# Next image's projection three steps later in a state-space loop, and attention's row-of-maxima matmuls issued pair by pair

## The chip, the cores and the metric

The kernel runs on one core of a Trainium2 chip. The metric is the device time of one execution in microseconds (us). The engines are TensorE (PE in the profile, its weight loads PEld), VectorE (DVE), ScalarE (ACT), GpSimd (POOL) and SyncE (SP), which here only issues DMAs. Each engine works through its own instruction stream and waits on counting semaphores.

## The reference

A tensor x of 16 images, 64 channels, 32x32 pixels passes four blocks. The change touches the first and the last.

```python
# block 0: transformer, 8 heads of 32, 1024 tokens per image
qkv = layer_norm(x_flat, g1, beta1) @ w_qkv.T
scores = jnp.einsum('bhqd,bhkd->bhqk', q, k) * HEAD_DIM ** (-0.5)
attn = jax.nn.softmax(scores, axis=-1)
out = jnp.einsum('bhqk,bhkd->bhqd', attn, v)
...
# blocks 1 and 2: two 3x3 convolutions with batch norm, then iterative whitening
...
# block 3: state space model, 128 channels, 16 states, L = 1024
xz = jnp.einsum('blc,ec->ble', xn, W_in); xi, z = jnp.split(xz, 2, axis=-1)
xc = jax.nn.silu(causal depthwise conv of xi, 4 taps)
dt, Bm, Cm = jnp.split(jnp.einsum('bld,ed->ble', xc, W_x), ...)
delta = jax.nn.softplus(dt @ W_dt.T + b_dt)
hst = hst * exp(d_t A) + (d_t * u_t) B_t;  y_t = sum over n of hst C_t
out = ((ys + xc * Dp) * silu(z)) @ W_out.T + x
```

## The kernel before

The program is a chain of phases, each a block with one hand-written stream for each engine. Two phases matter here: attention and state space.

**Attention.** The work is cut into 32 periods (16 images, two groups of four heads), each of 16 steps: two halves of 512 queries by eight blocks of 128 keys. A step works on a 128-key block and 512 queries for the four heads of a group. The heads lie on partitions 0-31, 32-63, 64-95 and 96-127, so a matmul of head h uses rows 32h to 32h+31 of TensorE's array. In step s TensorE issues:

- `scores` (lines 391 to 403): for each head the float32 product K·Q into PSUM tile `at_sc` (line 398; the profile records each such matmul as two passes), and then for each head a one-row bf16 matmul of ones by `at_nrow` (line 401), which adds the negated row maximum to all scores. Before head 0 it waits until the exponential of heads 0 and 1 of the step before is done (`exp_done`), and before head 2 for that of heads 2 and 3, since `at_sc` is not doubled. `sc_ready` is raised after the ones matmul of head 1 and again after that of head 3.
- `maxima`, heads 0 and 1 (line 334), which make bf16 scores for the maxima of a later group, in a ring of three PSUM banks that VectorE reduces (line 526);
- in some steps, other units in the same ring: projections of q and k (steps 0 and 1), the turning of maxima into rows (4 and 12), projections of v (6), softmax denominators (1 and 9);
- `values`, the product of the probabilities of step s-1 with V (line 410), and `maxima` of heads 2 and 3.

ScalarE takes the exponential of two heads at a time (line 479, `at_sc` to `at_probs`), first heads 0 and 1, then heads 2 and 3.

**State space.** Per image there are 16 steps n, one for each state. VectorE scans in two halves (lines 1587, 1591) and multiplies by the spread row of C (`see`, line 1599). TensorE spreads row n of C over 128 partitions (line 1411, PSUM tile `ss_C`, one buffer, so it waits for `see` of n-1) and adds the seen state of n-1 into `ss_Y` (line 1423). ScalarE makes the decay (line 1534), GpSimd the drive (line 1634).

The next image's inputs are made within the same 16 steps by four units of TensorE in `unit(b + 1, ...)`, each issued between the C row of step n and the `ss_Y` matmuls behind it. A table of step numbers (line 1278) sets where: `AT_X` for unit 0, the projection and convolution of the next image (line 1388, from `ss_xn` and `ss_w_taps` into PSUM tile `ss_aux`), and for ScalarE's `take_x` (line 1463), which copies it out; `AT_Z` (8) for unit 1, the gate (line 1393), `AT_BC` (9), `AT_DT` (12) and so on. `AT_CONV` is in the table but is read nowhere. Unit 0 waits for `xn_in`, the two DMAs of `ss_xn`. SyncE issues these in step `TURN` (3), behind the store of the image before, which waits for `res_done` of ScalarE in step 2:

```python
                if n == TURN:
                    sp.wait_ge(gate_done, b + 1)
                    load_x(b + 1)
```

Of the kernel before, what the change touches and what calls it, by code (L numbers as in the profile page):

```python
# [19 lines left out]
HEADS, DH = 8, 32  # L20
INNER = HEADS * DH
GH = P // DH
# [125 lines left out]
def attention_phase(nc, sem, xn_d, wqkvT, ident_bf, attn_d):  # L148
# [39 lines left out]
    def stage_before(stage, grp):  # L188
        if stage == "first":
            return "lead"  # L190
        return "first" if isinstance(grp, int) and grp == 1 else "mid"
# [7 lines left out]
    def unit_count(stage, grp, unit):  # L199
        is_max = unit[1] == "max"  # L200
        same = [u for u in UNITS[stage] if (u[1] == "max") == is_max]
        return counted_before(N_MAX if is_max else N_EXTRA, grp) + same.index(unit) + 1

    def unit_of(stage, kind, which, s=None):
        return next(u for u in UNITS[stage] if u[1:3] == (kind, which) and s in (None, u[0]))
# [12 lines left out]
    with ExitStack() as ctx:  # L218
# [6 lines left out]
        ones_bf = sb("at_ones_bf", [P, P], BF16)  # L225
# [9 lines left out]
        nrow = sb("at_nrow", [P, 2, HALF], BF16)  # L235
# [3 lines left out]
        sc = ps("at_sc", [P, GH, HALF])  # L239
# [10 lines left out]
        def hs(h):  # L250
            return slice(h * HALF, (h + 1) * HALF)

        def blk(k):
            return slice(k * P, (k + 1) * P)

        def head(h):
            return slice(h * DH, (h + 1) * DH)
# [54 lines left out]
        def _(pe):  # L312
# [76 lines left out]
            def scores(stage, grp, par, s):  # L389
                half, kb = divmod(s, KB)  # L390
                if kb == 0:

                    at = stage if half else stage_before(stage, grp)
                    pe.wait_ge(extra_done, unit_count(at, grp if half else grp - 1, unit_of(at, "turn", half)))
                for h in range(GH):
                    if h % 2 == 0 and not (stage == "first" and s == 0):
                        pe.wait_ge(exp_done, 2 * (STEPS * grp + s - 1) + h // 2 + 1)
                    nc.tensor.matmul(sc[:, h, :], KT[head(h), par, blk(kb)], QT[head(h), par, hs(half)], start=True, stop=False)  # L398
                for h in range(GH):
                    row = slice(h * DH, h * DH + 1)  # L400
                    m = nc.tensor.matmul(sc[:, h, :], ones_bf[row, :], nrow[row, half, :], start=False, stop=True)  # L401
                    if h % 2:
                        m.then_inc(sc_ready, 1)

            def values(grp, par, s):
# [8 lines left out]
            def period(grp, par, stage):  # L414
                for s in range(STEPS):
                    if stage != "lead":
                        scores(stage, grp, par, s)
                    maxima(stage, grp, par, s, (0, 1))
                    if s < 2:
                        project(stage, grp, par, s)  # L420
                    if s % KB == 1 and stage != "lead":
                        denominators(stage, grp, 1 - s // KB)
                    if s == 4 or s == 12:
                        turn(stage, grp, 1 if s == 4 else 0)
                    if s == 6:
                        values_projected(stage, grp, par)
                    if stage != "lead":
                        if s == 0:
                            if stage != "first":
                                values(grp - 1, 1 - par, STEPS - 1)  # L430
                        elif s % KB == 2:
                            values(grp, par, s - 2)
                            values(grp, par, s - 1)
                        elif s % KB != 1:
                            values(grp, par, s - 1)
                    maxima(stage, grp, par, s, (2, 3))
# [769 lines left out]
def state_space_phase(nc, sem, xn_d, xw_d, w_inT, conv_w, conv_b, w_xT, w_dtT, b_dt, a_log, d_p, w_outT,  # L1206
# [15 lines left out]
    with ExitStack() as ctx:  # L1222
# [52 lines left out]

        LEAD = DEPTH - 2

        AT_X, AT_CONV, AT_Z, AT_BC, AT_REST, AT_MID, AT_DT, AT_LOW, AT_DELTA = 3, 4, 8, 9, 10, 11, 12, 12, 13

        def loop_steps(b, par):  # L1280

# [389 lines left out]
def conv_transformer_ssm(nc, a, out):  # L1671

    with ExitStack() as ctx:
# [23 lines left out]
        with nc.sbuf_tensor("x_centred", [P, PAIRS, S], F32) as centred:  # L1697
            whitening_phase(nc, sem, x2_d, total, a["pair_m"], a["mask_m"], a["ident"], centred, wm)
            whiten_norm_phase(nc, sem, centred, wm, a["L2_conv_weight"], a["L2_conv_bias"], a["L3_conv_ln_w"],
                              a["L3_conv_ln_b"], a["mean_m"], xw_d, xm_d)  # L1700
        state_space_phase(nc, sem, xm_d, xw_d, a["L3_conv_W_in"], a["L3_conv_conv_w"], a["L3_conv_conv_b"],
                          a["L3_conv_W_x"], a["L3_conv_W_dt"], a["L3_conv_b_dt"], a["L3_conv_A_log"], a["L3_conv_Dp"],
                          a["L3_conv_W_out"], a["select_m"], a["ident"], rows_d, out.rearrange("n c h w -> n c (h w)"))
# [37 lines left out]
```

## Time and profile before

| | us |
|---|---|
| median of 3 runs | 3976.04 |
| lowest and highest | 3971.3 and 3979.86 |
| the profiled execution, own time | 3973.87 |
| its span (first to last instruction) | 3972.2 |
| TensorE busy | 3373.5 (85%) |
| VectorE busy | 2573.4 (65%) |
| ScalarE busy | 2001.1 (50%) |
| GpSimd busy | 1924.1 (48%) |

The busy time of TensorE counts overlapping matmuls once and stretches with a lower clock, so it does not say that the array is full. The mean granted clock of TensorE was 0.917 of the full 2.4 GHz.

### The profile page before, as it was taken

How to read it: one execution, taken by the hardware profiler on the slowest of the kernel's cores; microseconds unless marked ns; L12 is line 12 of the kernel's file. 1: busy time of each engine (PE TensorE's matmuls, PEld its weight loads, DVE VectorE, ACT ScalarE, POOL GpSimd, SP SyncE). 2: the span in 40 equal slices, each digit the busy share in tenths (PEclk: the TensorE clock that was granted, in tenths of full speed). 3: DMA queues.
4: the chain of work that ended last, by engine and by line, in shares of the span. 5: the costliest groups of instructions: out<-in, count | busy, mean ns of one | idle time of the engine just before them, and what ended most of it. 6: DMA issues, size and time to landing. Idle time of an engine off the chain costs nothing. (4 is left out here: it accounts for less than half of the span.)

```text
span 3972.2 us, 56517 instructions
## 1 busy us (share of the span) xinstructions
PE 3373.5 (85%) x19062; PEld 1207.9 (30%) x19062; DVE 2573.4 (65%) x3346; ACT 2001.1 (50%) x2381; POOL 1924.1 (48%) x620
## 2 busy tenths in 40 slices
PE   6999999999999999999995999657777777777777
PEld 2333333333333333333331333422222222222222
DVE  5677677676676776767750222237777777777777
ACT  3566566565565665656652333234454445444554
POOL 0555566555565655556653000016555655555555
PEclk7899999999999999999997999778888888888888
DMA  2000000000000000000003210134323332333242
GB/s 95 12 14 15 10 17 15 15 15 10 15 17 15 9 15 15 15 15 12 15 9 92 90 63 16 56 103 146 136 96 139 115 130 96 139 115 128 96 143 102
DMA packets 74768, 235.22 MB, mean 59 GB/s; under 512 B 13089, under 2 KB 14181, under 8 KB 74421
## 3 DMA queue, kind: packets, MB, share of 16 engines
q1 hardware_dynamic: 69460, 215.06, 16.0%
q0 software_dynamic: 5056, 16.83, 1.2%
q8 instruction: 155, 2.54, 0.3%
q14 instruction: 97, 0.79, 0.1%
HBM read 192.42 MB, written 39.39 MB: 58 GB/s over the span
## 5 line engine op out<-in xcount | busy, mean ns | idle before, releaser
L526 DVE TENSOR_REDUCE at_pmax<-at_ring 128x1 f32<-128x512 f32 x2048 | 1305.1, 685 | 512.5 <-PE at_ring L334 511.6
L479 ACT ACTIVATE at_probs<-at_sc 128x1024 f32<-128x1024 f32 x1024 | 992.5, 1021 | 660.4 <-PE at_sc L401 660.3
L580 POOL TENSOR_TENSOR at_prob_sums<-at_prob_sums,at_probs 128x2048 f32<-128x2048 f32 x192 | 869.3, 4527 | 109.7 <-ACT at_probs L479 98.7
L398 PE MATMUL at_sc<-at_QT,at_KT 32*128 32x512 f32 x4096 | 847.8, 642 | 21.9 <-issue 21.6
L1634 POOL TENSOR_TENSOR ss_drive<-ss_du,ss_bsb 128x1024 f32<-128x1024 f32 x261 | 610.0, 2350 | 424.9 <-DVE ss_state L1591 417.8
L580 POOL TENSOR_TENSOR at_prob_sums<-at_probs 128x2048 f32<-128x2048 f32 x64 | 291.0, 4547 | 791.2 <-ACT at_probs L479 791.2
L410 PE MATMUL at_O<-at_probs,at_V 128*32 128x512 f32 x4096 | 539.2, 610 | 53.0 <-DVE at_att L549 51.8
L1534 ACT ACTIVATE ss_decay<-ss_delta,ss_a 128x512 f32<-128x512 f32 x520 | 353.2, 687 | 441.8 <-DVE ss_state L1587 304.0
L1423 PE MATMUL ss_Y<-ss_seen,ss_ident 128*128 128x512 f32 x1032 | 540.1, 649 | 0.0
L1599 DVE TENSOR_TENSOR ss_seen<-ss_state,ss_C 128x1024 f32<-128x1024 f32 x259 | 316.3, 1221 | 256.4 <-PE ss_C L1411 249.8
L334 PE MATMUL at_ring<-at_KH,at_QH 32*128 32x512 bf16 x2048 | 447.4, 389 | 5.7 <-DVE at_pmax L526 2.9
L1591 DVE TENSOR_TENSOR_SCAN ss_state<-ss_decay,ss_state,ss_drive 128x512 f32<-128x512 f32 x259 | 332.2, 1283 | 31.5
L401 PE MATMUL at_sc<-at_nrow,at_ones_bf 1*128 1x512 bf16 x2048 | 339.5, 381 | 0.0
L1587 DVE TENSOR_TENSOR_SCAN ss_state<-ss_decay,ss_drive 128x512 f32<-128x512 f32 x259 | 314.8, 1215 | 22.3 <-POOL ss_drive L1634 15.8
L398 PEld LDWEIGHTS at_sc<-at_QT,at_KT 32*128 32x128 f32 x4096 | 274.9, 186 | 176.2 <-ACT at_probs L479 149.2
L1411 PE MATMUL ss_C<-ss_bc,ss_select 96*128 96x512 bf16 x518 | 167.0, 406 | 188.6 <-DVE ss_seen L1599 187.5
L334 PEld LDWEIGHTS at_ring<-at_KH,at_QH 32*128 32x128 bf16 x2048 | 150.9, 92 | 534.1 <-DVE at_pmax L526 342.9
L1423 PEld LDWEIGHTS ss_Y<-ss_seen,ss_ident 128*128 128x128 f32 x1032 | 208.4, 206 | 241.2 <-issue 192.0
L1388 PE MATMUL ss_aux<-ss_xn,ss_w_taps 128*128 128x512 f32 x136 | 104.7, 941 | 109.6 <-DMA ss_xn<-scratch_xm 108.6
L385 PE MATMUL at_ring<-at_probs,at_ones 128*32 128x512 f32 x1512 | 175.3, 596 | 1.4 <-DVE at_pmax L526 1.4
L938 POOL DMA_DIRECT2D scratch_x<-fc_out x8 | 4.3, 534 | 351.6 <-ACT fc_out L839 351.6
L410 PEld LDWEIGHTS at_O<-at_probs,at_V 128*32 128x32 f32 x4096 | 87.6, 108 | 273.2 <-issue 189.3
(199 smaller groups left out, 2728.2 us busy)
## 6 DMA issues: line engine op xcount, KB each, us to landing
ss_bsb<-scratch_rows SPq DMA_DIRECT2D x265, 512.0 KB, 6.8
scratch_attn<-at_att SPq DMA_DIRECT2D x64, 256.0 KB, 2.0
fc_att<-scratch_attn SPq DMA_DIRECT2D x32, 512.0 KB, 5.8
ss_xn<-scratch_xm SPq DMA_DIRECT2D x34, 256.0 KB, 5.5
at_xn<-scratch_xn SPq DMA_DIRECT2D x32, 256.0 KB, 3.8
ss_xw<-scratch_xw SPq DMA_DIRECT2D x17, 256.0 KB, 3.7
ln_x<-in_x SPq DMA_DIRECT2D x8, 512.0 KB, 4.4
scratch_xn<-ln_xn POOLq DMA_DIRECT2D x8, 512.0 KB, 3.0
```

The lines of the kernel that those rows point to most:

```text
L334: nc.tensor.matmul(ring[:, unit[3], :], QH[head(h), p, blk(quad // 2)], KH[head(h), p, hs(quad % 2)], start=True, stop=True).then_inc(max_ ...
L398: nc.tensor.matmul(sc[:, h, :], KT[head(h), par, blk(kb)], QT[head(h), par, hs(half)], start=True, stop=False)
L401: m = nc.tensor.matmul(sc[:, h, :], ones_bf[row, :], nrow[row, half, :], start=False, stop=True)
L410: m = nc.tensor.matmul(O[head(h), :], V[:, par, kb, head(h)], probs[:, kb, h, :], start=(kb == 0), stop=(kb == KB - 1))
L479: nc.scalar.activation(probs[:, kb, two, :].rearrange("p h q -> p (h q)"), sc[:, two, :].rearrange("p h q -> p (h q)"), ACT.Exp, scale=SCA ...
L526: nc.vector.tensor_reduce(pmax[:, quad // 2, h, quad % 2:quad % 2 + 1], ring[:, unit[3], :], AX_X, ALU.max, negate=True).then_inc(max_done, 1)
L580: nc.gpsimd.tensor_tensor(prob_sums[:, half, :, :], before, probs[:, k, :, :], ALU.add).then_inc(pool_sums, 1)
L1423: m = nc.tensor.matmul(Y[:, hs(h)], ident[:], seen[:, n % DEPTH, hs(h)], start=False, stop=(n == N - 1))
L1534: nc.scalar.activation(decay[:, hs(h)], delta[:, par, hs(h)], ACT.Exp, scale=a_neg[:, n:n + 1])\
L1591: nc.vector.tensor_tensor_scan(now[:, hs(1)], decay[:, hs(1)], drive[:, n % DEPTH, hs(1)], now[:, HALF - 1:HALF], ALU.mult, ALU.add).then_ ...
L1599: nc.vector.tensor_tensor(seen[:, n % DEPTH, :], state[:, n % 2, :], Cp[:], ALU.mult).then_inc(seen_done, 1)
L1634: nc.gpsimd.tensor_tensor(drive[:, n % DEPTH, :], du[:, par, :], bsb[:, n % SLOTS, :], ALU.mult).then_inc(drive_done, 1)
```

## The change

In attention, the ones matmuls of heads 0 and 1 are issued right behind the scores of heads 0 and 1, ahead of the wait for heads 2 and 3 and of their scores; before, all four came behind all four scores. In the state space phase, `AT_X` goes from 3 to 6: unit 0 of TensorE and `take_x` of ScalarE for the next image move three steps later. `AT_CONV` changes too, without effect. SyncE's stream is the same.

```diff
                     if h % 2 == 0 and not (stage == "first" and s == 0):
                         pe.wait_ge(exp_done, 2 * (STEPS * grp + s - 1) + h // 2 + 1)
                     nc.tensor.matmul(sc[:, h, :], KT[head(h), par, blk(kb)], QT[head(h), par, hs(half)], start=True, stop=False)
-                for h in range(GH):
-                    row = slice(h * DH, h * DH + 1)
-                    m = nc.tensor.matmul(sc[:, h, :], ones_bf[row, :], nrow[row, half, :], start=False, stop=True)
                     if h % 2:
+                        for of in (h - 1, h):
+                            row = slice(of * DH, of * DH + 1)
+                            m = nc.tensor.matmul(sc[:, of, :], ones_bf[row, :], nrow[row, half, :], start=False, stop=True)
                         m.then_inc(sc_ready, 1)
...
-        AT_X, AT_CONV, AT_Z, AT_BC, AT_REST, AT_MID, AT_DT, AT_LOW, AT_DELTA = 3, 4, 8, 9, 10, 11, 12, 12, 13
+        AT_X, AT_CONV, AT_Z, AT_BC, AT_REST, AT_MID, AT_DT, AT_LOW, AT_DELTA = 6, 6, 8, 9, 10, 11, 12, 12, 13
```

TensorE's stream in attention, the steps around an early period's turning unit, as it was (`at_sc` is scores, `at_ring` the ring, `at_O` the output):

```order
38 L401 MATMUL at_sc<-at_nrow,at_ones_bf 128x512 x4
39 L334 MATMUL at_ring<-at_KH,at_QH 128x512 x2
40 L410 MATMUL at_O<-at_probs,at_V 32x512 x4
41 L334 MATMUL at_ring<-at_KH,at_QH 128x512 x2
42 L398 MATMUL at_sc<-at_QT,at_KT 128x512 x4
43 L401 MATMUL at_sc<-at_nrow,at_ones_bf 128x512 x4
44 L334 MATMUL at_ring<-at_KH,at_QH 128x512 x2
45 L372 MATMUL at_ring<-at_ident,at_negm 128x128 x4
```

The same place of TensorE's stream with the change:

```order
46 L402 MATMUL at_sc<-at_nrow,at_ones_bf 128x512 x2
47 L334 MATMUL at_ring<-at_KH,at_QH 128x512 x2
48 L410 MATMUL at_O<-at_probs,at_V 32x512 x4
49 L334 MATMUL at_ring<-at_KH,at_QH 128x512 x2
50 L398 MATMUL at_sc<-at_QT,at_KT 128x512 x2
51 L402 MATMUL at_sc<-at_nrow,at_ones_bf 128x512 x2
52 L398 MATMUL at_sc<-at_QT,at_KT 128x512 x2
53 L402 MATMUL at_sc<-at_nrow,at_ones_bf 128x512 x2
54 L334 MATMUL at_ring<-at_KH,at_QH 128x512 x2
55 L372 MATMUL at_ring<-at_ident,at_negm 128x128 x4
```

The number of matmuls is the same; two ones matmuls moved ahead of two scores.

TensorE's stream in the state space loop, from step 2 of an image to step 5, as it was (`ss_aux<-ss_xn,ss_w_taps` is unit 0):

```order
1539 L1423 MATMUL ss_Y<-ss_seen,ss_ident 128x512 x2
1540 L1429 REGISTER_ALU
1541 L1411 MATMUL ss_C<-ss_bc,ss_select 128x512 x2
1542 L1381 ISA
1543 L1388 MATMUL ss_aux<-ss_xn,ss_w_taps 128x512 x4
1544 L1423 MATMUL ss_Y<-ss_seen,ss_ident 128x512 x2
1545 L1429 REGISTER_ALU
1546 L1411 MATMUL ss_C<-ss_bc,ss_select 128x512 x2
1547 L1423 MATMUL ss_Y<-ss_seen,ss_ident 128x512 x2
```

The place where unit 0 now stands in TensorE's stream, steps 6 to 8 of the same image, with unit 1 (`ss_aux<-ss_xn,ss_w_in`) behind it:

```order
1742 L1411 MATMUL ss_C<-ss_bc,ss_select 128x512 x2
1743 L1381 ISA
1744 L1388 MATMUL ss_aux<-ss_xn,ss_w_taps 128x512 x4
1745 L1423 MATMUL ss_Y<-ss_seen,ss_ident 128x512 x2
1746 L1429 REGISTER_ALU
1747 L1411 MATMUL ss_C<-ss_bc,ss_select 128x512 x2
1748 L1423 MATMUL ss_Y<-ss_seen,ss_ident 128x512 x2
1749 L1429 REGISTER_ALU
1750 L1411 MATMUL ss_C<-ss_bc,ss_select 128x512 x2
1751 L1393 MATMUL ss_aux<-ss_xn,ss_w_in 128x512 x2
```

Unit 0 has moved behind three more pairs of C row and `ss_Y`; ScalarE's `take_x` moves past three steps of decays in the same way.

## Rows read from the trace of the kernel before

**Rows 1.** Busy time by window: attention, then state space; clock and DMA last.

```profile
core 0: us, PE busy (x) PEld busy (x) DVE busy (x) ACT busy (x) POOL busy (x), PEclk, DMA share, GB/s
95.00:2120.00 2025.00, 1917.06 (x15294) 672.51 (x15293) 1401.30 (x2261) 1194.00 (x1402) 1160.28 (x256) 0.98 0.04 14
2640.00:3972.00 1332.00, 986.57 (x2096) 353.94 (x2096) 982.51 (x817) 616.42 (x778) 725.97 (x312) 0.85 0.35 120
```

**Rows 2.** Waits in state space: total us, times, longest.

```profile
DVE ss_seen L1599 <- PE ss_C L1411: 244.4, 67, 10.6
PE ss_aux L1388 <- DMA ss_xn<-scratch_xm: 108.6, 15, 7.7
```

**Rows 3.** Timeline of one image around step 3: start, us, engine, instruction, idle before.

```profile
3251.15 0.60 PE L1411 MATMUL ss_C<-ss_bc,ss_select 96*128 96x512 bf16 x2
3252.30 1.12 SPq L1291 DMA_DIRECT2D ss_xn<-scratch_xm  x2
...
3259.13 6.34 PE L1388 MATMUL ss_aux<-ss_xn,ss_w_taps 128*128 128x512 f32 x8 [7.38 <-DMA ss_xn<-scratch_xm]
...
3267.02 0.60 PE L1411 MATMUL ss_C<-ss_bc,ss_select 96*128 96x512 bf16 x2
...
3267.72 1.22 DVE L1599 TENSOR_TENSOR ss_seen<-ss_state,ss_C 128x1024 f32<-128x1024 f32 x1 [10.47 <-PE ss_C L1411]
```

**Rows 4.** The first and the last such stall of VectorE, of 15.

```profile
2793.42 1.22 DVE L1599 TENSOR_TENSOR ss_seen<-ss_state,ss_C 128x1024 f32<-128x1024 f32 x1 [10.16 <-PE ss_C L1411]
...
3902.36 1.22 DVE L1599 TENSOR_TENSOR ss_seen<-ss_state,ss_C 128x1024 f32<-128x1024 f32 x1 [10.36 <-PE ss_C L1411]
```

**Rows 5.** Timeline of undisturbed steps, and unit 1 in step 8.

```profile
3275.30 1.22 DVE L1599 TENSOR_TENSOR ss_seen<-ss_state,ss_C 128x1024 f32<-128x1024 f32 x1
...
3279.10 1.22 DVE L1599 TENSOR_TENSOR ss_seen<-ss_state,ss_C 128x1024 f32<-128x1024 f32 x1
...
3280.91 3.20 PE L1393 MATMUL ss_aux<-ss_xn,ss_w_in 64*128 64x512 f32 x4
```

**Rows 6.** Timeline of the first image, whose `ss_xn` had landed before step 3.

```profile
2708.07 3.60 PE L1388 MATMUL ss_aux<-ss_xn,ss_w_taps 128*128 128x512 f32 x8
...
2711.51 1.88 PE L1423 MATMUL ss_Y<-ss_seen,ss_ident 128*128 128x512 f32 x4
...
2713.92 1.22 DVE L1599 TENSOR_TENSOR ss_seen<-ss_state,ss_C 128x1024 f32<-128x1024 f32 x1 [0.19 <-PE ss_C L1411]
```

**Rows 7.** Busy time by window after the stall; the granted clock is the number behind POOL.

```profile
3264.50:3281.50 17.00, 12.77 (x35) 5.01 (x34) 13.27 (x11) 6.47 (x10) 7.05 (x3) 1.00 0.06 22
3281.60:3288.30 6.70, 6.70 (x10) 1.89 (x8) 4.89 (x4) 5.93 (x7) 3.91 (x2) 0.50 0.00 0
```

**Rows 8.** Waits in attention: total us, times, longest.

```profile
ACT at_probs L479 <- PE at_sc L401: 623.6, 423, 9.3
```

**Rows 9.** Timeline of step 15 of an attention period.

```profile
1045.75 1.94 ACT L479 ACTIVATE at_probs<-at_sc 128x1024 f32<-128x1024 f32 x2 [1.24 <-PE at_sc L401]
...
1046.83 1.60 PE L398 MATMUL at_sc<-at_QT,at_KT 32*128 32x512 f32 x6
1047.73 0.19 PEld L398 LDWEIGHTS at_sc<-at_QT,at_KT 32*128 32x128 f32 x2 [0.60 <-ACT at_probs L479]
...
1047.80 0.38 PE L401 MATMUL at_sc<-at_nrow,at_ones_bf 1*128 1x512 bf16 x2
...
1048.27 0.59 PE L398 MATMUL at_sc<-at_QT,at_KT 32*128 32x512 f32 x2
...
1048.93 1.94 ACT L479 ACTIVATE at_probs<-at_sc 128x1024 f32<-128x1024 f32 x2 [1.24 <-PE at_sc L401]
```

**Rows 10.** Timeline of step 3, in which nothing makes TensorE wait.

```profile
1034.82 1.24 PE L398 MATMUL at_sc<-at_QT,at_KT 32*128 32x512 f32 x8
...
1036.20 1.94 ACT L479 ACTIVATE at_probs<-at_sc 128x1024 f32<-128x1024 f32 x2 [2.31 <-PE at_sc L401]
```

**Rows 11.** First scores of one period and of the next: the first and last of 17 starts.

```profile
1050.01 0.70 PE L398 MATMUL at_sc<-at_QT,at_KT 32*128 32x512 f32 x2
...
1111.47 0.70 PE L398 MATMUL at_sc<-at_QT,at_KT 32*128 32x512 f32 x2
```

## The prediction

> **What bounds the kernel now.** I first cut the span into stages [rows 1]: attention takes 2025 us, state space 1332 us, and each is half of the change. Then I read in each the list of waits and one timeline.
>
> State space. The list of waits shows VectorE waiting 244.4 us for the C row of TensorE, longest 10.6, and TensorE waiting 108.6 us in 15 waits for the DMA of `ss_xn` [rows 2]. The timeline joins the two [rows 3]. In step 3 the C row is out at 3251.15; next in the stream stands unit 0, and its data are asked for only at 3252.30. They land at 3259.13, after 7.38 us of an idle TensorE. The unit then takes 6.34 us. Only behind it and the `ss_Y` matmuls comes the next C row (3267.02), for which VectorE has sat 10.47 us. Undisturbed steps are 3.80 us apart (3275.30 to 3279.10) [rows 5], and there VectorE is the bound, with next to no gap. So a step of VectorE is the unit of time of this stage, and once an image 10.2 to 10.5 us are added. The first and the last stall show 10.16 and 10.36 [rows 4]; there are 15 of them, one for each image but the first. The sum of the 15 excesses over 3.80, from one first-half scan to the next, is 154 us (15 x 10.27).
>
> Attention. ScalarE waits 623.6 us for the ones matmuls, 423 times [rows 8]. A step is a closed loop [rows 9]. Let t be the start of the scores of head 0, u the start of those of head 2, e the start of the first exponential. The exponential of the step before starts at 1045.75, and u comes 1.98 later (1047.73), when its second half has freed the banks. The scores of heads 2 and 3 end at 1048.27 + 0.59 = 1048.86, and e is 1048.93, u + 1.20. But the ones matmuls of heads 0 and 1, all that the first exponential needs, had started at 1047.80 and ended at 1048.18. It is released 0.75 us later, right behind the last score, which stands ahead of them in program order: I read that ends are reported in program order. The loop is u to e 1.20, e to u 1.98: 3.18 us, the distance of the two ACT rows, with ScalarE idle for 1.24. Where TensorE never waits, e is 1.38 behind t (1034.82 to 1036.20) [rows 10].
>
> **Part 1, state space.** Nothing is added; unit 0 moves. At 3.80 us a step, see 3 starting at 3253.5 puts the C row of step 6 at about 3262.3 and the unit at 3262.8, against data landed at 3259.13: 3.7 us to spare, and the longest wait (7.7) [rows 2] is only 0.3 above the one shown. The DMA wait goes. SyncE's queue is unchanged, and so are the stores and row spreads behind the load.
>
> What is left is the unit's own work in a step whose bound is VectorE. The trace has this case: in the first image `ss_xn` had landed before step 3 [rows 6]. There the unit took 3.60 us, the `ss_Y` matmuls 1.88, and VectorE's next but one `see` waited 0.19 us. The step was 0.14 longer. So at full clock the stall costs 0.14 instead of 10.27.
>
> The clock is the unknown. Behind the stall the clock was 0.50 and the unit took 6.34 instead of 3.60; then 1.00 for 17 us of undisturbed steps, and 0.50 again for 6.7 us from 3281.6, over unit 1 (3.20 us) [rows 5, 7]. TensorE had then been through a few undisturbed steps, in which it pauses for VectorE (12.77 us busy of 17), since its last dense stretch; a unit in step 6 stands behind three such steps too. So I take one chance in two that a 6.8 us dip falls on it. Such a dip takes away half of its length in streaming, 3.4 us, of which 0.1 is slack: 3.3. Some of that returns, as the same dip no longer falls on units 1 and 2. I take 1.1 us net per image. Bounds: 0 (all at full clock) and 6.34 - 3.60 + 1.9 for `ss_Y` at half clock + 0.3 = 4.9 (none). Saved: 15 x (10.27 - 0.14 - 1.1) = 135 us; bounds 152 and 78.
>
> ScalarE's `take_x` moves too; ScalarE is busy for 6.47 of those 17 us [rows 7], and in the first image the same copy beside the same decays is inside the 0.14.
>
> **Part 2, attention.** No instruction is added. With the ones matmuls of heads 0 and 1 ahead of the scores of heads 2 and 3, the first exponential starts at t + 1.39 whatever u is, if ends are reported in order; and u of the next step becomes t + 1.39 + 1.98 = t + 3.37 to 3.39, where it was u + 3.18. What TensorE needs from u to the next t stays: 2.28 us in a plain step (1047.73 to 1050.01) [rows 9, 11], more where other units stand. Write d = u - t (0.90 now in plain steps; at least 0.22, since head 2 runs behind the maxima of heads 2 and 3) and w for the stretch from u to the next t. Then the step is d + w, and the next d is the larger of 0.22 and 3.39 - (d + w). Over the period shown, 1050.01 to 1111.47 = 61.46 us, the sixteen w, from the seventeen starts of which these are the first and last, are 4.48, 6.75, 4.02, 2.46, 2.85, 2.28, 4.26, 2.28, 2.28, 4.86, 4.03, 2.46, 2.85, 2.28, 2.28, 2.28: together 52.7. The d are 0.90, 0.22 three times, 0.70, 0.33, 0.90, 0.22, 0.88, 0.90, 0.22, 0.22, 0.70, 0.33, 0.90, 0.90: 8.76. By the rule the d become 0.89, 0.22 three times, 0.71, 0.22, 0.89, 0.22, 0.89, 0.22 three times, 0.71, 0.22, 0.89, 0.22: 7.18. A run of plain steps alternates 2.50 and 3.17, mean 2.83 instead of 3.18, but most of the period lies in steps that TensorE's other units set, where nothing is won. Saved: 1.58 us a period, 32 periods: 51 us. Next in line is TensorE itself, busy with w. Bounds: 0, with the loss as a rival below, and 64: w may shrink where it holds waits on the ring that ScalarE's earlier finish shortens; I allow 0.4 a period, 32 x 1.98.
>
> **Sum.** 135 + 51 = 186 off the profiled execution's own time, 3973.9 (2.2 below the median): 3788; with the 2 us of the median, 3790.
>
> **Rivals.**
>
> - *Attention slower than before.* Program order could hold starts as well as ends: the scores of head 2 would then start only behind the ones matmul of head 1, 0.97 behind t. With d never under 0.97 the period is 52.7 + 15.5 = 68.2, +6.8 x 32 = +216, less 135: 4055. It decides from d of about 0.8 in every step (+134). Against it: the ones matmuls that started at 1047.80 stand in program order behind the second passes of heads 2 and 3, which started at 1048.27 [rows 9]; different row groups overtake each other. Chance 0.04.
> The Trainium skill, page "TensorE: Matmul & The Clock Gate", section "The mechanism", has matmuls strictly first in, first out in start and end. By its rule for starts this rival would happen, and the time would be the one given above. The trace agrees with the rule for ends (released at 1048.93, not 1048.18) and contradicts that for starts (1047.80 before 1048.27), so the rows decide.
> - *Attention gains nothing.* A milder form: the weight load of the scores of head 2 queues behind that of the ones matmul, which waits for the second pass of head 0, about 0.54 behind t (as 1048.27 is behind 1047.73 for head 2). With d at least 0.55 the period is 61.5: no gain. For it: no row shows a ones load pending ahead of an unstarted score. Against it: loads of later rows in other row groups did go ahead. Total 3841. Chance 0.13.
> - *Half clock in most units 0*, or DMA lands late in some images: state space saves 78 to 100; total 3825 to 3850. Chance 0.10.
> - *The stall only moves.* If the loads were pushed back with the step, unit 0 would stall as before. The loads are issued in step 3 as before, so only 0.02, at 3920.
> - Both parts as costed: 0.71, and then 3760 to 3815.
>
> **How the numbers follow.** The likeliest is 3790. Best bounds together give 3976 - 152 - 65 = 3759. Upwards the range takes in the second and third rival, to 3855; what is left out is the first and fourth rival and mixtures, about 1 to 2 in 10. Below 3968 (0.2%, about what a measurement of this kernel can tell from no change) lie all but the first rival and half of the fourth: faster 0.94, same 0.01, slower 0.05.
>
> **What would show it.** In the changed trace TensorE has no wait for `ss_xn`; the row of `ss_seen` behind the C row falls from 244 us to about 100 (244 less 154, and what the clock adds); unit 0 takes 3.6 us where the clock is 1.00. In attention ScalarE's gap in plain steps alternates around 0.9 instead of 1.24, and the distance of periods is 59.9. A load of head 2's scores that starts only with or behind the ones matmul of head 0 would prove me wrong there; dips of the clock on every unit 0 would do so in the state space.

## The result, and the profile after

The changed kernel takes 3751.49 us (median of 4 runs, 3748.16 to 3760.68) against 3974.7 us before: a ratio of 0.9441 (of the means), 95% interval 0.942 to 0.9462. That is 223 us, where 186 was forecast; 3751 lies 8 us under 3759, the forecast's best bounds taken together. The direction and both mechanisms were right, the size of the state space part was not.

By window, the stages of [rows 1]: attention, then the state space loop. The columns are the same.

```profile
core 0: us, PE busy (x) PEld busy (x) DVE busy (x) ACT busy (x) POOL busy (x), PEclk, DMA share, GB/s
95.00:2062.00 1967.00, 1850.22 (x15294) 692.82 (x15293) 1400.97 (x2260) 1198.56 (x1402) 1160.34 (x256) 0.98 0.04 14
...
2630.00:3740.00 1110.00, 897.30 (x2057) 326.02 (x2058) 976.55 (x807) 597.90 (x757) 716.09 (x308) 0.93 0.40 137
```

VectorE is busy for 976.55 of 1110 us of the loop, as long as before in a shorter loop; the granted clock rises from 0.85 to 0.93.

The profiled execution (span 3746.7 us, 225.5 less) divides as follows, each from the trace's starts and ends: up to the last work on attention's tiles 2121.1 before, 2063.1 after (-58.0); from there to the first scan of the state space loop 573.6 and 565.1 (-8.5); from the first scan to the last 1265.7 and 1108.5 (-157.2); the tail behind it gives the last 1.8.

The timeline around unit 0 in the state space loop, the answer to [rows 3, 6]:

```profile
2986.33 1.12 SPq L1291 DMA_DIRECT2D ss_xn<-scratch_xm  x2
2987.52 1.22 DVE L1599 TENSOR_TENSOR ss_seen<-ss_state,ss_C 128x1024 f32<-128x1024 f32 x1
...
2991.32 1.22 DVE L1599 TENSOR_TENSOR ss_seen<-ss_state,ss_C 128x1024 f32<-128x1024 f32 x1
...
2995.11 1.22 DVE L1599 TENSOR_TENSOR ss_seen<-ss_state,ss_C 128x1024 f32<-128x1024 f32 x1
...
2996.83 3.60 PE L1388 MATMUL ss_aux<-ss_xn,ss_w_taps 128*128 128x512 f32 x8
...
2998.91 1.22 DVE L1599 TENSOR_TENSOR ss_seen<-ss_state,ss_C 128x1024 f32<-128x1024 f32 x1
...
3002.70 1.22 DVE L1599 TENSOR_TENSOR ss_seen<-ss_state,ss_C 128x1024 f32<-128x1024 f32 x1
```

The loads are issued at the same place, just ahead of `see` of step 3. TensorE comes to unit 0 10.5 us later without a wait, the unit takes 3.60 us, and VectorE's `see` rows stay 3.79 to 3.80 apart straight through it. It costs nothing.

The answers to [rows 5, 7] on the clock are the rows of units 0 and 1 over the loop (lowest, median and highest duration in ns of one matmul pass):

```profile
L1388 PE MATMUL ss_aux<-ss_xn,ss_w_taps x120: 590/592/595, 2720.1 to 3689.5; 128*128 128x512 f32 x120
```

```profile
L1393 PE MATMUL ss_aux<-ss_xn,ss_w_in x60: 587/590/693, 2727.9 to 3695.7; 64*128 64x512 f32 x60
```

The same rows of the kernel before read 1061 and 696 in the middle and 1222 and 1057 at the top. The rows leave out the loop's first image, whose two units take 3.60 and 1.99 us. So no unit 0 and no unit 1 of the loop meets half clock any more.

Attention, step 14 and the start of step 15 of a period, the answer to [rows 9, 10]:

```profile
1075.93 1.57 PE L398 MATMUL at_sc<-at_QT,at_KT 32*128 32x512 f32 x6
...
1076.80 0.19 PEld L398 LDWEIGHTS at_sc<-at_QT,at_KT 32*128 32x128 f32 x2 [0.24 <-ACT at_probs L479]
1076.89 0.38 PE L402 MATMUL at_sc<-at_nrow,at_ones_bf 1*128 1x512 bf16 x2
...
1077.31 1.94 ACT L479 ACTIVATE at_probs<-at_sc 128x1024 f32<-128x1024 f32 x2 [0.56 <-PE at_sc L402]
1077.34 0.59 PE L398 MATMUL at_sc<-at_QT,at_KT 32*128 32x512 f32 x2
...
1079.08 0.52 PEld L398 LDWEIGHTS at_sc<-at_QT,at_KT 32*128 32x128 f32 x8
1079.08 1.35 PE L398 MATMUL at_sc<-at_QT,at_KT 32*128 32x512 f32 x8
1079.62 0.32 PEld L402 LDWEIGHTS at_sc<-at_nrow,at_ones_bf 1*128 1x128 bf16 x4
...
1080.46 1.94 ACT L479 ACTIVATE at_probs<-at_sc 128x1024 f32<-128x1024 f32 x2 [1.22 <-PE at_sc L402]
```

The exponential at 1077.31 starts 1.38 behind t (1075.93) although the second passes of heads 2 and 3 start only at 1077.34: it no longer waits for them. Their first passes are the last two of the six in the row at 1075.93, which ends at 1077.50; head 2's load stands at 1076.80, ahead of the ones rows of heads 0 and 1 at 1076.89, which precede it in program order. The ones rows end at 1077.27 and the exponential starts 0.04 later, while head 2's first pass is still running. The step is 3.15 long and the next 2.50 (1079.08 to 1081.58), the alternation of the forecast. The eight loads of all scores stand ahead of the first load of a ones row (1079.62), although two ones rows precede heads 2 and 3 in program order. A period is 59.90 us [rows 11: 61.46]:

```profile
1021.68 0.70 PE L398 MATMUL at_sc<-at_QT,at_KT 32*128 32x512 f32 x2
...
1081.58 0.70 PE L398 MATMUL at_sc<-at_QT,at_KT 32*128 32x512 f32 x2
```

### The profile page after: what moved, and what is told of

Its sections match the earlier page's. It is cut to its first block and busy times, and to the rows that moved or that the text cites. A ratio compares the mean times of both kernels' runs of the same rounds, so it can differ in the third digit from the quotient of the medians.

```text
span 3746.7 us, 56517 instructions
## 1 busy us (share of the span) xinstructions
PE 3233.9 (86%) x19062; PEld 1206.6 (32%) x19062; DVE 2573.4 (69%) x3346; ACT 2006.2 (54%) x2381; POOL 1925.2 (51%) x620
## 5 line engine op out<-in xcount | busy, mean ns | idle before, releaser
L398 PE MATMUL at_sc<-at_QT,at_KT 32*128 32x512 f32 x4096 | 781.2, 636 | 21.6 <-issue 21.2
L1423 PE MATMUL ss_Y<-ss_seen,ss_ident 128*128 128x512 f32 x1032 | 523.1, 631 | 0.0
L402 PE MATMUL at_sc<-at_nrow,at_ones_bf 1*128 1x512 bf16 x2048 | 315.7, 380 | 0.0
L398 PEld LDWEIGHTS at_sc<-at_QT,at_KT 32*128 32x128 f32 x4096 | 257.0, 185 | 68.1 <-ACT at_probs L479 39.6
L1411 PEld LDWEIGHTS ss_C<-ss_bc,ss_select 96*128 96x128 bf16 x518 | 40.5, 101 | 383.7 <-DVE ss_seen L1599 319.4
```

The costliest lines, as they stand in the source:

```text
L1423: m = nc.tensor.matmul(Y[:, hs(h)], ident[:], seen[:, n % DEPTH, hs(h)], start=False, stop=(n == N - 1))
```

## The experiments

All times stand beside runs of the kernel before on the same chip: 3972.32 us for the first four, 3976.48 for the next four, 3974.14 for the last three.

**One part at a time.** State space part alone:

```diff
-        AT_X, AT_CONV, AT_Z, ... = 3, 4, 8, ...
+        AT_X, AT_CONV, AT_Z, ... = 6, 6, 8, ...
```

> Only unit 0 and take_x moved from step 3 to step 6; attention as before. Theory A (the parts add up, and the stretch between the two phases owes nothing to either): the time is about 158 us under before, 3817, with the stall of step 4 gone (154 us) and every unit 0 and unit 1 at full clock. Theory B (part of the state space saving came from the clock left by a faster attention): less than 145 saved, over 3830, and units 1 at half clock in several images.

Measured: 3810.65 us, ratio 0.9587 (0.9564 to 0.961); first to last scan 1108.5 us, as with both parts; all sixteen units 0 of the loop 3.60 us and all units 1 1.98 or 1.99. Theory A: the loop gains the same with attention as it was.

The attention part alone (`scores` as in the change, the table as before):

> Only the ones matmuls moved ahead; the state space loop as before. Theory A (the parts add up): a period of 59.9 us instead of 61.5, and about 58 us less in all, 3917; the state space stage keeps its 15 stalls of 10.3 us. Theory B (the 9 us that the phases between attention and state space also lost belong to this part): 66 us less, 3909.

Measured: 3922.74 us, ratio 0.9874 (0.9841 to 0.9906). The median period is 59.90 and attention ends at 2063.9, so this stage gains what it gains with both parts, 57 us. The state space stage keeps its stalls, 215.2 us of steps against 214.9, and takes 1272.8 us where the kernel before had 1265.7 in its profile: 7 us more, all of it in steps whose length hangs on the clock. The stretch between is 571.7, so theory B's price is not there. The product of the two ratios is 0.9466, and both together gave 0.9441: within the intervals they add up. In the median this part alone gave 50 us, where 58 was expected; the 7 us that the loop lost account for most of that.

**Is it the place or the wait?** Unit 0 stays in step 3; the loads come earlier in SyncE's stream, ahead of the wait for the output store.

```diff
             def step(b, par, n):
...
-                if n == TURN:
-                    sp.wait_ge(gate_done, b + 1)
-                    load_x(b + 1)
             def between(b, par):
+                sp.wait_ge(gate_done, b + 2)
+                load_x(b + 2)
                 store(b)
```

(with the first load ahead of the loop, and one more image in the scratch tensor for the load past the end)

> Kernel before, unit 0 still in step 3, but the loads of the image after next are issued at the end of step 2's issues, ahead of the wait for the output store, so that they have landed before step 3. Theory A (the stall was the landing time, and the dips of the clock on units 1 in step 8 were a consequence of the stall): the step behind step 3 falls from 14.1 to 3.8 to 4.0 us, no unit 1 runs at half clock, and the time is 150 to 160 under before, as with the move to step 6. Theory B (the dips in step 8 come from the undisturbed steps before them): unit 1 is still at half clock in half of the images, and the time is 10 to 15 us higher than in theory A. Theory C (the place in the step matters, the output matmuls of step 1 just ahead of unit 0 delay the C row): 15 x 1 to 2 us more than theory A.

Measured: 3807.06 us, ratio 0.9577 (0.9554 to 0.96). From first to last scan 1102.1 us, 163.6 less than before and 6 less than with the later step. The step of the stall takes 3.95 us (63.2 for 16). The rows of units 0 and 1 from the second image on:

```profile
L1390 PE MATMUL ss_aux<-ss_xn,ss_w_taps x120: 590/592/595, 2780.5 to 3739.1; 128*128 128x512 f32 x120
```

```profile
L1395 PE MATMUL ss_aux<-ss_xn,ss_w_in x60: 587/590/693, 2799.6 to 3756.5; 64*128 64x512 f32 x60
```

The first image's unit 1 is the exception:

```profile
2727.26 3.02 PE L1395 MATMUL ss_aux<-ss_xn,ss_w_in 64*128 64x512 f32 x4
```

The stall was the landing time, as theory A says. On the clock theory A holds in fifteen images of sixteen. In the kernel before, unit 1 ran partly at half clock in eleven of sixteen images: in ten of the fifteen with a stall, and in the first, which has none. Here one is left, though the same undisturbed steps 4 to 7 precede the unit in every image. So those steps alone do not bring the dip, and taking the stall away moved it off unit 1 in this kernel. It did not do so in every kernel, as the last experiments show.

**Where the landing time bites.** The changed kernel with unit 0 in step 4, and in step 5 (`AT_X, AT_CONV = 4, 4` and `5, 5`), beside the changed kernel itself.

> The changed kernel with unit 0 and take_x in step 4. TensorE reaches the unit at about 4.4 us behind the C row of step 3 and the data land 8 us behind it. Theory A (only the landing time counts): TensorE waits about 3.9 us, VectorE is 3.7 us late once an image, 15 x 3.7 = 56 us over the changed kernel. Theory B (the wait also costs the clock, as the 7.4 us wait did): unit 0 at half clock, up to 4.7 us more an image, 100 to 126 us over, and dips on units 1 in step 8 come back.

Measured: 3898.77 us, 142 over the changed kernel beside it (3756.69). One of its stalls:

```profile
2809.61 6.24 PE L1388 MATMUL ss_aux<-ss_xn,ss_w_taps 128*128 128x512 f32 x8 [3.67 <-DMA ss_xn<-scratch_xm]
...
2827.49 2.89 PE L1393 MATMUL ss_aux<-ss_xn,ss_w_in 64*128 64x512 f32 x4
```

The wait is the 3.7 us that was foreseen, 55.7 us over the fifteen images. But the step behind it takes 157.8 us over 16 images instead of 60.7 (+97, 6.5 each), since most of the unit runs at half clock (6.24 for 3.60); steps 9 and 10 cost 20 more (all sixteen units 1 partly at half clock), steps 2 and 13 21 more. Theory B, and past its upper price: what the clock costs, 41 us in that step and 41 in the other four, is more than the wait.

> The changed kernel with unit 0 and take_x in step 5. TensorE reaches the unit 8.2 us behind the C row of step 3, just about when the data land. Theory A (only the landing time counts): within 5 us of the changed kernel. Theory B (a place this tight is missed in some images): 10 to 30 us over, with waits for the DMA of a microsecond in several images.

Measured: 3763.84 us (3755.91 to 3776.47), 7 over. The step behind unit 0 takes 71.4 us for 16 (+10.7): one unit 0 takes 6.74 us and one 5.40, the others 3.60 to 3.70, with waits of TensorE's weight loads for the DMA of up to 2.3 us. Between the theories, nearer to B in kind and to A in size: at step 5 a margin of nothing is missed a few times. The 7 us are less than the spread of its four runs, but the 10.7 us stand in the trace.

> The changed kernel itself, for comparison with the three kernels beside it on the same chip. 3751 us, with the parts as before: a period of attention 59.9 us, 1108 us from the first to the last scan. The stretch between the last attention matmul and the first scan was 565 us here and 572 to 575 in the other kernels: if it is 572 to 575 this time, that difference is chance and not an effect of the change.

Measured: 3756.69 us, ratio 0.9447 (0.9424 to 0.947); first to last scan 1109.2, the stretch between the phases 570.4.

**Both early.** Early loads, unit 0 in step 3, and the attention part:

> The attention part of the change together with the early loads, unit 0 left in step 3. If the two parts add up, this is the changed kernel less the 4 to 6 us by which the early loads beat the later step: 3742 to 3748 us, and unit 0 at full clock in all images but none with a dip in steps 4 to 11.

Measured: 3754.61 us (3744.3 to 3757.63), ratio 0.9442 (0.9419 to 0.9465). From first to last scan 1101.9, 7 less than the changed kernel beside it, so the parts add up in the profile; in the medians the difference (2 us) is too small to tell, and 3742 to 3748 had been expected. That no dip would fall in steps 4 to 11 missed in two images: units 1 of the first two take 3.15 and 3.02 us.

**In what order are ends reported?** Attention alone, with the ones rows of heads 0 and 1 between the scores of head 2 and those of head 3:

```diff
                     nc.tensor.matmul(sc[:, h, :], KT[head(h), par, blk(kb)], QT[head(h), par, hs(half)], start=True, stop=False)
+                    if h >= 2:
+                        ones_rows(h - 2)   # ones matmuls of heads 2*(h-2), 2*(h-2)+1, then sc_ready
```

> Attention alone changed: the ones matmuls of head 0 and 1 stand behind the scores of head 2 and ahead of those of head 3, so they are released for ScalarE by the count raised after head 1's, now with one score matmul ahead of it in program order. State space as before. Theory A (ends are reported in program order): the first exponential again starts 1.2 us behind the start of head 2's scores, the period is back at 61.4 us and the time at 3965 to 3975, that is within 0.3% of before. Theory B (what counts is that the ones matmuls get through early, ahead of head 3's scores and of the end of the eight): a good part of the 58 us stays, 3920 to 3945.

Measured: 3975.78 us, ratio 1.0002 (0.9986 to 1.0017), median period 61.41.

```profile
1044.58 1.59 PE L404 MATMUL at_sc<-at_QT,at_KT 32*128 32x512 f32 x6
1045.54 0.38 PE L398 MATMUL at_sc<-at_nrow,at_ones_bf 1*128 1x512 bf16 x2
...
1045.99 0.60 PE L404 MATMUL at_sc<-at_QT,at_KT 32*128 32x512 f32 x2
...
1046.63 1.94 ACT L482 ACTIVATE at_probs<-at_sc 128x1024 f32<-128x1024 f32 x2 [1.23 <-PE at_sc L398]
```

Here L398 is the ones row. It ends at 1045.92 and is released at 1046.63, just behind the end of the row at 1045.99 (1046.59), which holds the second passes of heads 2 and 3. Only head 2's score stands ahead of the ones rows in program order. That a count waits for every matmul that is under way is ruled out by the changed kernel, where it came at 1077.31, while head 2's pass ran on to 1077.50. One score matmul ahead in program order is enough to take back nearly the whole gain (61.41 against 61.54 from the same rows of the kernel before). Theory A.

**The pause that is left.** After the change a dip lies over unit 3 in step 12 of every image, behind a pause of 2.59 us; six images have a second, shorter one around step 1. The changed kernel, and the one with both parts early, with two more matmuls (`ss_zero`, all zeros) into `ss_Y` in step 11; they compute nothing:

```diff
                         add_state(*before)
+                        if now[2] == 11:
+                            for h in range(2):
+                                nc.tensor.matmul(Y[:, hs(h)], zero[:], seen[:, before[2] % DEPTH, hs(h)], start=False, stop=False)
```

> The changed kernel, with two more matmuls per image that add zero times the seen state to ss_Y, in step 11 behind the ss_Y matmuls, where TensorE pauses for 2.6 us. What they compute is zero and the output is the reference's. Theory A (the dip of the clock at step 12 of each image is a consequence of that pause, as the dip at step 3 was of the DMA wait): most dips at step 12 go, unit 3 takes 2.0 us instead of 3.0 to 3.8, the step behind step 12 falls from 5.8 towards 4.3, and the time is 15 to 30 us under the changed kernel (3725 to 3740). Theory B (it comes from something else, or the extra 1.7 us of matmuls are too few): the dips stay and the time is within 5 us.

Measured: 3753.15 us, ratio 0.9449 (0.943 to 0.9467); the changed kernel beside it 3757.52. Step 12 in the changed kernel:

```profile
3021.36 0.61 PE L1411 MATMUL ss_C<-ss_bc,ss_select 96*128 96x512 bf16 x2 [2.59 <-DVE ss_seen L1599]
3021.90 3.42 PE L1405 MATMUL ss_aux<-ss_dt,ss_w_dt 4*128 4x512 f32 x4
```

And with the filler:

```profile
3030.96 1.88 PE L1453 MATMUL ss_Y<-ss_seen,ss_zero 128*128 128x512 f32 x4
3033.71 0.60 PE L1414 MATMUL ss_C<-ss_bc,ss_select 96*128 96x512 bf16 x2 [0.87 <-DVE ss_seen L1606]
3034.25 1.98 PE L1408 MATMUL ss_aux<-ss_dt,ss_w_dt 4*128 4x512 f32 x4
```

All sixteen units 3 of the loop take 1.98 us, and the step behind them falls from 97.2 to 69.5 us over 16 images. So unit 3's dip hangs on the pause in this kernel. A pause there does not always bring it: in the kernel before, TensorE pauses for 2.41 or 2.59 us in every image, and six of the sixteen units 3, all behind 2.41, run at full clock. And dips of 3.4 us come elsewhere: in fifteen images one over the `ss_Y` matmuls of step 1, for which step 2 grows from 101.5 to 117.7, and in the last six another that starts just behind unit 3 and costs nothing. The loop gains 11 us (1109.3 to 1098.0), the median 4, which the intervals do not tell from nothing. In the profiled executions the loop's gain is used up elsewhere: attention ends 5.6 us later (2068.8 for 2063.2) and the stretch between takes 7.3 more (574.6 for 567.3), both with the same code. Cause as in theory A, time as in theory B.

> The kernel with early loads, unit 0 in step 3 and the attention part of the change, with the same two matmuls in step 11. As for the filler in the changed kernel; if both work as in theory A, the fastest of all, 3715 to 3735.

Measured: 3749.33 us (3747.97 to 3750.95), ratio 0.9437 (0.9421 to 0.9453): the lowest of the medians, and 14 us over the top of the forecast. First to last scan 1098.6, only 3 us less than without the filler. Step 13 gains 22.5 us (92.0 to 69.5 over 16 images), step 2 loses 11.6 (94.2 to 105.8), and steps 9 and 10 lose 7.4 (159.5 to 166.9), since eight of the sixteen units 1 run partly at half clock. One of them, and the busy times and clock (0.50) of the window of its dip:

```profile
2875.76 0.61 PE L1416 MATMUL ss_C<-ss_bc,ss_select 96*128 96x512 bf16 x2 [1.47 <-DVE ss_seen L1608]
2876.30 2.78 PE L1398 MATMUL ss_aux<-ss_xn,ss_w_in 64*128 64x512 f32 x4
```

```profile
2877.40:2884.10 6.70, 6.70 (x10) 1.78 (x9) 4.85 (x5) 5.92 (x7) 4.34 (x2) 0.50 0.00 0
```

No image of this kernel has a stall, and no wait of TensorE in the loop is longer than 1.8 us. So a dip on unit 1 does not need the stall.

> The changed kernel once more, on the chip of the two filler kernels. 3751 to 3757 us; the stretch from the last attention matmul to the first scan, 565 and 570 us in its two profiles so far, between 565 and 575.

Measured: 3757.52 us, ratio 0.9463 (0.9445 to 0.9481); the stretch between the phases 567.3.

## Why the prediction was right and wrong

**What bound the stages: right.** The stall stood where it was read. Taking the DMA wait away by other means (early loads) gives 164 us, against 157 for moving the unit.

**State space, the stall: right.** The step behind it falls from 214.9 us over 16 images to 60.7, 154.2 less; forecast 154 less 2 for the 0.14 per image. The 0.14 was read from the first image, the one without a stall. It returned with unit 0 in step 3 and early loads (3.95 us) and is nought in step 6. In step 3 the output matmuls of step 2 leave TensorE no pause ahead of the C row; in step 6 it pauses for 1.47 us there.

**State space, the clock: the step that failed.** The prediction said "I take one chance in two that a 6.8 us dip falls on it", and charged 1.1 us net per image, 16 us. No dip fell on any unit 0: with the unit in step 6, all 80 units of five profiles take 3.60 us, but for one of 3.68. I had read the dip on unit 1 as the work of the three undisturbed steps before it, and carried it to step 6, which has three such steps before it as well. The run with early loads has those same steps before unit 1, without the stall, and a dip in one image of sixteen; with unit 0 in step 6 unit 1 meets none in 80. So those steps do not suffice. What does bring the dip stays open. It was rare once the stall was gone, but with early loads and the filler it fell on eight units 1 of sixteen without any stall, and with the filler and unit 0 in step 6 on none. So the place of the dense unit 0, two steps ahead of unit 1 or five, seems to matter as well as the stall. What went and came in the time is measured: with the change, steps 9 and 10 gave 12.8 us (169.7 to 156.9 over 16 images). Against that, dips over step 12 and step 1 grew a little more frequent or longer, and steps 2 and 13 lost 9.8 (188.0 to 197.8). The net is +3 instead of -16, and with the 2 us of the 0.14 the loop saved 157.2 where 135 was said, past the bound of 152. That bound assumed that the best case is "no dip on unit 0", and left out that dips on other units can go too.

**Attention: right in its mechanism and in its period.** 59.90 was forecast and measured. Inside, two steps differ and cancel: step 0 takes 5.10 where 5.37 was said and step 9 5.42 where 5.08 was said. In step 0 ScalarE's copy of q starts 3.31 us behind t instead of 3.93, and what waits for its bank of the ring comes sooner. In step 9 TensorE now comes to the denominators before the bank is free and waits 0.28 us for VectorE:

```profile
1059.37 2.78 PE L385 MATMUL at_ring<-at_probs,at_ones 128*32 128x512 f32 x24 [0.28 <-DVE at_pmax L526]
```

Here taking work away from one wait brought out another, and that the two steps cancel is luck. The stage gained 58.0 instead of 51: 31 periods, from one first exponential to the next, sum to 1951.9 us before and 1895.6 after, 56.3 less. Of these 31 x 1.56 = 48.4 are the plain gain. The other 8 come from longer periods, nearly all of them the first two and those with or behind a clock dip. In the trace the clock is at half for 10.2 us every fourth period before, for 6.8 after. Why they are shorter was not tried.

**The stretch between** was not in the sum, and gave 8.5 us in the profiled execution. Its code is the same in all kernels. It took 573.6 in the kernel before; 565.1, 570.4 and 567.3 in three profiles of the changed kernel; 571.7 to 575.1 in the kernels with one part; and 565.3 to 574.6 in the others with both. So it varies by 10 us with no clear owner, and the 8.5 us cannot be put down to the change. That it goes with where dips fall was not tried.

**The rivals.** Starts in program order: refuted by head 2's load at 1076.80, ahead of the ones rows at 1076.89, and by the time. The milder form, a score's load queued behind a ones load: refuted by the loads at 1079.08, since all eight score loads precede the first ones load. Late DMA or half clock on most units: absent in step 6; in step 5 two units of sixteen run at half clock, and in step 4 fifteen. The stall only moves: no.

**The sum.** In the profiled executions 225.5 us were gained, 39.5 more than forecast: 22 of these come from the state space loop, 7 from attention, 8.5 from the stretch between and 2 from the tail. The two best bounds together reached only 31 us below the likeliest; the larger, 152 for the loop, was too tight (157.2), and for the stretch there was no bound at all. The stretch helped by chance, as far as the runs tell; the step that was priced wrongly is the clock.

## What to carry to other kernels

A wait of TensorE can cost more than its length: with unit 0 in step 4, waits of 55.7 us in sum cost 142. Where a trace shows one, add the half-clock work behind it, and when it goes, count that as gained too. Dips some steps away belong in the range and not in the sum: they left with the stall in most of these kernels, and in one they were back without it. For the order within TensorE's stream, ask two separate questions: what can start (other row groups overtake), and what can be reported (nothing overtakes); a count that another engine waits for belongs ahead of every matmul that it does not need. When data land late, moving the consumer and moving the load are worth the same; leave some microseconds of margin, since at none it was missed in single images.

## What the runs showed of the hardware

- The end of a matmul is reported to a waiting engine in program order, even across row groups: with one score ahead of it a ones row that ended at 1045.92 was released at 1046.63, and with none ahead one that ended at 1077.27 was released at 1077.31. The Trainium skill, page "TensorE: Matmul & The Clock Gate", section "The mechanism", says so of ends, and the runs agree; what it says of starts does not hold here, as the ones row at 1045.54 stands behind head 2's score in program order but ahead of the second pass of that score at 1045.99.
- A wait of TensorE of 3.7 us left the clock at half for most of the unit behind it (6.24 us for 3.60), and the unit 18 us later ran partly at half clock too (2.89 for 1.98). In the changed kernel, whose longest wait in the loop is 2.59 us, the clock stayed full from step 3 to step 11 of every image; with early loads and the filler, whose longest is 1.8 us, it fell to half over unit 1 in eight images of sixteen.
- Filling the 2.59 us pause of step 11 with 1.9 us of matmuls brought unit 3 behind it to full clock in all sixteen images. Shorter dips came elsewhere, in fifteen images over step 1.
